# Moving eight score tiles of the third head group to later steps of the first group, in two causal attention cores

## The reference

```python
scores = jnp.einsum('bqhd,bkhd->bhqk', q, k)
scores = jnp.where(causal_mask[None, None], scores, NEG)
attn = jax.nn.softmax(scores, axis=-1)
out = jnp.einsum('bhqk,bkhd->bqhd', attn, v).reshape(b, s, HIDDEN)
```

## Time and profile before

| what | value |
| --- | --- |
| median of 3 runs | 2194.98 us (2193.35 to 2201.15) |
| profiled execution, its own time | 2201.1 us |
| its span, first to last instruction | 2199.3 us |
| PE busy | 2024.1 us (92%) |
| DVE busy | 1212.7 us (55%) |
| ACT busy | 894.8 us (41%) |
| POOL busy | 698.0 us (32%) |
| mean granted clock of PE | 0.962 of full speed |
| score tiles of `first` on DVE | 173.2 to 400.2 us |
| score tiles of `rotary` on DVE | 1188.0 to 1414.0 us |

### The profile page before, as it was taken

How to read it: one execution, slowest core, us unless ns; L and a number is a source line. 1 busy time by engine, 2 the same in 40 slices (tenths; PEclk the granted TensorE clock), 3 DMA queues, 4 the chain that set the end, 5 groups by cost and what they waited for, 6 DMA issues and landing times.

```text
span 2199.3 us, 31486 instructions
## 1 busy us (share of the span) xinstructions
PE 2024.1 (92%) x10679; PEld 1354.8 (62%) x10679; DVE 1212.7 (55%) x2649; ACT 894.8 (41%) x1695; POOL 698.0 (32%) x610
## 2 busy tenths in 40 slices
PE   7997999978799999997998999978999999999998
PEld 6775666666433334335776566656888787555664
DVE  6454656467799898876776666535323153121221
ACT  3424545355377676773543544534212211111111
POOL 0004655346423232323664655501000000223332
PEclk9998999989799999998998999998999999999999
DMA  5738766357764645443567766452112045233331
GB/s 196 227 144 169 157 147 146 104 192 252 236 147 114 148 115 146 98 125 120 205 204 204 167 154 153 110 216 96 44 53 75 3 180 222 55 65 62 63 61 36
DMA packets 150834, 297.67 MB, mean 135 GB/s; under 512 B 24594, under 2 KB 43156, under 8 KB 149588
## 3 DMA queue, kind: packets, MB, share of 16 engines
q1 hardware_dynamic: 112900, 242.29, 38.2%
q10 hardware_dynamic: 29040, 34.74, 6.2%
q0 software_dynamic: 8736, 18.62, 4.5%
HBM read 181.55 MB, written 102.50 MB: 129 GB/s over the span
## 4 chain that ended last, share of the span: by engine, by line
PE 41%; DMA 5%; DVE 3%; issue 1%; POOL 1%; ACT 1%; SPq 1%; DVEq 0%; POOLq 0%; ACTq 0%
PE bank L1840 10%; PE bank L1928 8%; PE bank L1851 5%; PE bank L1947 4%; PE bank L515 2%; PE bank L1155 2%; PE bank L1189 2%; PE bank L1247 2%; PE bank L1230 2%; DMA stack<-rotary_c_max_rows 1%; DMA normed<-xt 1%; PE bank L1198 1%; PE bank L1912 1%; DMA xt<-normed,moe_row_at 1%; DVE rotary_p_hn L743 1%
## 5 line engine op out<-in xcount | busy, mean ns | idle before, releaser
L1336 ACT ACTIVATE cross_c_prob<-bank 128x512 f32<-128x512 f32 x512 | 271.1, 598 | 118.4 <-PE bank L1189 117.1
L1386 DVE TENSOR_REDUCE row_max<-bank 128x2 f32<-128x1024 f32 x248 | 290.8, 1212 | 29.3 <-PE bank L1155 28.3
L1840 PE MATMUL bank<-moe_hT,moe_w 128*128 128x512 f32 x1056 | 251.8, 394 | 17.8 <-DVE moe_prod L2207 11.5
L1189 PE MATMUL bank<-stack 56*128 56x512 f32 (+4 forms) x768 | 234.6, 430 | 13.7 <-DMA stack<-first_c_max_rows 4.4
L1840 PEld LDWEIGHTS bank<-moe_hT,moe_w 128*128 128x128 f32 x1056 | 200.0, 190 | 61.0 <-DVE moe_prod L2207 11.9
L1155 PE MATMUL bank<-stack 48*128 48x512 f32 (+4 forms) x720 | 191.0, 445 | 25.1 <-PEq L71 13.9
L1189 PEld LDWEIGHTS bank<-stack 56*128 56x128 f32 (+1 forms) x768 | 119.2, 194 | 144.2 <-ACT cross_c_prob L1336 70.1
L1928 PE MATMUL bank<-moe_w_e,moe_hT_e 128*128 x624 | 194.4, 465 | 4.4 <-DMA moe_w_e<-in_experts_packed 3.9
L1928 PEld LDWEIGHTS bank<-moe_w_e,moe_hT_e 128*128 128x128 f32 x624 | 116.3, 191 | 65.9 <-issue 8.2
L1336 ACT ACTIVATE first_c_prob<-bank 128x512 f32<-128x512 f32 (+3 forms) x256 | 106.1, 437 | 124.3 <-PE bank L1192 121.8
L1336 ACT ACTIVATE rotary_c_prob<-bank 128x512 f32<-128x512 f32 (+3 forms) x256 | 106.0, 437 | 122.5 <-PE bank L1192 119.3
(11 more groups left out here) (391 smaller groups left out, 4051.5 us busy)
## 6 DMA issues: line engine op xcount, KB each, us to landing
moe_w_e<-in_experts_packed SPq DMA_DIRECT2D x8, 2176.0 KB, 8.8
qk_parts<-first_p_parts SPq DMA_DIRECT2D x32, 512.0 KB, 2.7
stack<-qk_parts SPq DMA_DIRECT2D x64, 256.0 KB, 6.5
qk_parts<-cross_p_parts SPq DMA_DIRECT2D x32, 512.0 KB, 2.7
stack<-qk_parts SPq DMA_DIRECT2D x256, 64.0 KB, 2.7
qk_parts<-rotary_p_parts SPq DMA_DIRECT2D x32, 512.0 KB, 2.8
moe_raw<-in_shared_packed SPq DMA_DIRECT2D x11, 768.0 KB, 10.5
stack<-qk_parts SPq DMA_DIRECT2D x16, 512.0 KB, 5.4
```

Of the source, the lines that this page charges most:

```text
L1189: last = nc.tensor.matmul(bank[:, 0 : S - q0], k_stack[slot][r : r + ALL_ROWS, at, m * P : (m + 1) * P], q_stack[slot][r : r + ALL_ROWS, a ...
L1336: nc.scalar.activation(probability(g, step // HEADS_AT_ONCE, step % HEADS_AT_ONCE), psum[bank_at["score", n]][:, 0 : S - q0], ACT.Exp).the ...
L1386: nc.vector.tensor_reduce(row_max[:, g % 2, m, j - 1 : j + 1], c.banks[:, first : first + WIDE, :], AX_X, ALU.max).then_inc(s.max_done, 1)
L1840: last = nc.tensor.matmul(psum[bank][:], weights(pa, f, k), hT[p % 2][:, pb, k, :], start=m == 0, stop=m == len(steps) - 1)
```

## The change

In group 0 of the causal cores, steps 6 to 9 make no score tile, and steps 10 to 13 make two each: step 10 tiles 0 and 1 of group 2, step 11 tiles 2 and 3, step 12 tiles 4 and 5, step 13 tiles 6 and 7. Steps 14 and 15 make tiles 8 and 9 as before. PE's loop and DVE's loop read the same table, so the order of the tiles, their banks and their counts stay. All other groups, and the cross core, keep their order. No transfer is added, removed or moved in its queue.

```diff
-        def scores_before(step):
+        HELD = {6: (), 7: (), 8: (), 9: (), 10: (6, 7), 11: (8, 9), 12: (10, 11), 13: (12, 13)}
+
+        def steps_of_tiles(g, step):
+
+            return HELD.get(step, (step,)) if causal and g == 0 else (step,)
+
+        def scores_before(g, step):
 
             if cross:
                 return range(step - 2, step + 2) if step % HEADS_AT_ONCE == 2 else ()
-            return (step,)
+            return steps_of_tiles(g, step)
...
-                            for ahead in scores_before(step):
+                            for ahead in scores_before(g, step):
                                 if tile_ahead(g, ahead):
                                     scores(*tile_ahead(g, ahead))
...
-                            if tile_ahead(g, step):
-                                tile_max(*tile_ahead(g, step))
+                            for ahead in steps_of_tiles(g, step):
+                                if tile_ahead(g, ahead):
+                                    tile_max(*tile_ahead(g, ahead))
```

## The result

The changed kernel takes 2204.97 us (median of 12 runs, 2201.88 to 2215.73), the kernel before 2196.68 us in the same session (12 runs, 2193.35 to 2202.95). The ratio is 1.0037, with a 95% interval of 1.0022 to 1.0051: slower by some 8 us, which is measurable and small. The profiled execution took 2203.75 us, its span is 2202.0.

What follows compares the result with a forecast made beforehand. Bound: arrival of group 1's maxima, held back by PE's stop for the stack of group 2. Gains of 4.7 us (first core) and 4.6 (rotary), together 9.3, from the median 2194.98 gave 2185.7, stated as 2185.5; range 2180 to 2191.

Steps and rivals of the forecast that it cites:

- The bound of group 1: Start of group 1 in the causal cores: set by when the row maxima arrive, not by PE's remaining tiles.
- The transposes: PE's transposes of group 1's maxima, first core: begin at 183.49, 1.51 us after step 5 ends.
- the maxima left: Sending of group 1's maxima: 4.91 us earlier in the first core, 4.69 us in the rotary core.
- PE was ready for group 1: PE's own work before group 1, first core: done between 191.3 and 193.3, with the maxima arriving at 191.5.
- The wait for the stack: Step 10, stack of group 2: wait covered by other work, by 0.6 us or more first core, 0.5 rotary.
- the way of the maxima: Group 1's maxima, sending to arrival: still 6.31 us in the first core and 6.64 in the rotary core.
- The lower bound of 5.15: Shortest time allowed for the maxima's way: 5.15 us, the quickest the chain shows later.
- the stack's own 10.77 us: Upper bound for the maxima's way: a stack transfer's own time in the same backlog.
- a rival with a chance of 0.05: Maxima as slow as the stacks, clock falling in the first core too: 2 us slower, 2197; chance 0.05.
- The rule of the Trainium skill: DMA engines alternate between queues packet by packet, so the maxima would not stand behind all SP has queued.
- The forecast of an undiminished shift: After group 1: everything hangs on the core's own steps, so the 9.3 us shift should arrive whole.

Runs made afterwards that it cites:

- e1: Changed kernel with the stack of group 3 issued in causal cores only after ten exponentials of group 0, behind the maxima's sending; time level with the kernel before.
- e11: Changed kernel once more with no edit, for a second profile; its own time is not given.
- e4: Changed kernel plus four products nobody reads, ahead of group 1 in each causal core; median 3.6 us under the changed kernel's, ratio interval 0.9980 to 1.0041.
- e5: Changed kernel with the stacks of groups 3 and 4 issued behind the maxima and the output weights asked for at step 9 of group 1; ratio 1.0016.
- e6: Kernel before, score tiles in their old order, with the same three later transfers as e5; ratio 1.0053.
- e8: Changed kernel with e5's late stacks, weights asked for in group 2, split in group 3, two residual blocks loaded in group 4; 2203.13 us, ratio 1.0015.
- e9: Kernel before, score tiles in their old order, with the same transfers as e8; 2219.68 us.

## Why the prediction was wrong

**What held.** The bound of group 1 was named rightly: the arrival of the maxima, not PE's work. The transposes came 1.49 us behind step 5 (forecast 1.51), the maxima left at 3.20 (3.22), in both cores. PE was ready for group 1 at 9.6 and 9.4 us (forecast 9.3 to 11.3). The wait for the stack was covered in the rotary core. In the first core 1.15 us were left, since values and sums went faster than I had them (the clock rose at 184) and the stack came 0.9 us later; it cost nothing, because the maxima came later still.

**The step that failed** is the way of the maxima: "I take the 6.3 and 6.6, since they too were sent into a share of about 1". They took 10.5 and 10.2. The premise was true only of the moment of sending (0.89 in the stretch at 191): over the 6.3 us of that way the mean share was 0.74, and over the 10.5 us now it is 1.09. A DMA share of 1.0 says that the engines are busy, and nothing of how much is queued ahead. When the maxima were sent at 190 before, SP's 3 MB were within 3 us of their end; 5 us earlier there were 8 us of it left. A wait for work that is already in line does not get shorter by joining the line sooner: the maxima arrived 0.8 and 1.2 us sooner, not 4.9 and 4.7, and against the second profile of the kernel before, where they arrive at 13.5 and 13.1, no sooner at all. e1 shows it by taking 1.5 MB out of the line: 3.4 and 3.2 us. The lower bound of 5.15 was not the quickest way either: the maxima of group 3, sent at 219.05 in the trace of the kernel before, took 3.1 us. The row for the slow way was there, the stack's own 10.77 us in the same backlog, and I had taken it as the bound of a rival with a chance of 0.05. That rival, slower than before by late maxima and a fall of the clock in the first core, is what happened in the profile. Its size is another matter: it said 2 us, and the two profiled spans differ by 2.7, but that is luck of these two executions, since the medians differ by 8.3.

**The rule of the Trainium skill** that I had weighed ("DMA: Bandwidth & Descriptors", Queues, rings and completion order: engines go round between the queues a packet at a time) would have let the first packet of the maxima through soon after the sending. It came 6.9 and 6.7 us later, when SP's packets thinned out, by ACT's queue and by POOL's alike. Here the measurement decides against that reading. A strict order of issue does not fit either, since the values' packets overtook the maxima's in e11; the runs don't show at which point of the way the line is.

**Where 8 us came from.** Most of it fits the clock. From the start of group 1 to that of group 4 the eight attention cores in the two profiles of each kernel took

```
us at 1.2 GHz in it      0     3.4   10.2   11.7   12.7   17.1   23.2   39.2
us from group 1 to 4   39.1   40.8   43.7   44.5   44.7   46.3   48.2   55.6
kernel               before before before changed changed before changed changed
```

which is, within 0.8 us, one line, 39 us and about 0.43 for each us at the lower clock, whichever the kernel. Before had 0 to 17.1 us of it (mean 7.7), the changed kernel 11.7 to 39.2 (mean 21.7): 5.8 us more a core, less 0.7 for the earlier start of group 1, and for two cores 10 us, beside the 8.3 of the medians. Of the 86.8 us of the four cores, 49 lie behind the stop for the maxima of group 1. The 23.9 behind POOL's stop are one core of one execution; without them the two cores come to 5 us.

The clocks of all executions allow an estimate that does not hang on four profiles. The mean granted clock was 0.9588 in 21 executions of the changed kernel and 0.9610 in 90 of the kernel before, which is some 10 us more at 1.2 GHz in an execution. Between step 5 and group 1 the profiles of the changed kernel have less of it, 5.1 us a core against 9.8. So, if the other stages have as much of it in both kernels, there are about 20 us more from group 1 on, and at 0.43 each, less the 0.7 a core, that is some 7 us of the 8.3.

The Trainium skill ("TensorE: Matmul & The Clock Gate", HAM oscillation — how this bites in real kernels) tells of transfers' waits after which the clock comes down and the next tile starts cold; the trace agrees, with a fall behind each of the four stops of 3.9 to 5.0 us and none behind the 0.96. What stays open is the size of it execution by execution: a stop of 2.3 us in the second profile of before was followed by 17 us of lower clock, and e4, which kept the clock up in group 1, had a median only 3.6 us lower, with another fall behind its next stop.

**The forecast of an undiminished shift** ("Nothing with a fixed time of its own stands in between") was the second error, smaller because there was hardly a shift. e1 had one of 5.1 and 4.2 us, and by group 4 (57.4 and 56.4, against a mean of 56.6 in the two profiles of the kernel before) all of it was spent: PE's two new stops, for the stack of group 3 and for the maxima of group 2, are 6.1 and 5.3 us together. The stacks of groups 2 to 4 and the weights are 5.5 MB, by an estimate 27 us of transfers at the 200 GB/s of the stretches, and an earlier start finds the same bytes in front of it. With the late transfers (e5 against e6, e8 against e9) the new order of the tiles is the faster one, but against the kernel before only the loss is made good.

## What to carry to other kernels

Before a small transfer on the critical path is sent sooner, count the bytes issued ahead of it: if they take longer than the send is moved, it arrives when it did, and the engine stands idle for it all the same. Look also at the clock where a stop lies. PE's 4.0 us for the stack, before, lay in a stretch that was at 1.2 GHz already (0.50 at 184); the change moved a stop of the same length to a place at 2.4 GHz, and the clock fell behind it, so that the work that followed paid. And a profile from one execution may contain a fall that the next has not: two profiles of the kernel before differed by 2.6 us of group 4's start in one core and 2.0 in the other.

## What the runs showed of the hardware

- A transfer of 64 KB had landed 3.2 to 3.4 us behind its sending with no stack queued ahead of it, at a mean DMA share of 0.42 to 0.48 over that time (e1), and 10.2 to 10.5 us behind it at 1.09, with a stack of 1.5 MB queued ahead on another queue. Its first packet moved 1.5 and 1.4 us behind the sending in e1, and 6.9 and 6.7 us with the stack ahead.
- Sending it by POOL's queue made no difference (PE starts group 1 at 14.1 and 13.3 us against 13.7 and 13.4).
- Packets of a transfer sent 2.2 us later on the same queue moved 0.9 us before its first one (e11).
- The share is no measure of the bytes: in the changed kernel it was 0.85 at 76 GB/s (stretch at 184), 1.11 at 180 (192) and 1.13 at 249 (195). Why the rate differs so is not shown.
